# GpSimd's queue order between norm offsets and residual additions in a Strassen-Winograd SwiGLU block on Trainium2

## The reference, cut to what matters

```
xn = layernorm(x)                                  # rows of 1024
q, k, v = xn@Wq, xn@Wk, xn@Wv                      # 64 wide
g = sigmoid(xn@Wg + bg)
S = decay*S + (k*g) (v*g)^T ; o = q@S ; s = o@Wo   # recurrence over the rows
gate, up = xn@Wgate.T/127, xn@Wup.T/127            # 3072 wide
ffn = (silu(gate)*up) @ Wdown.T/127                # back to 1024
out = x + s * silu(ffn)
```

## Time and profile before

| what | value |
|---|---|
| time, median of the runs | 534.76 us |
| lowest time | 533.02 us |
| time of the profiled execution | 532.67 us |
| span of its slowest core, 6 | 531.1 us |
| spans of the others | 526.7 (core 4) to 530.3 us (core 3) |
| TensorE (PE) busy | 505.8 us, 95% of the span |
| VectorE (DVE) busy | 359.9 us, 68% |
| ScalarE (ACT) busy | 189.2 us, 36% |
| GpSimd (POOL) busy | 122.2 us, 23% |

### The profile page before, as it was taken

One profiled execution on the slowest core, in us unless ns is written; L12 is line 12 of the kernel. 1 busy time (PEld: TensorE's weight loads), 2 busy tenths in 40 slices (PEclk: granted clock), 3 DMA queues, 4 the chain that ended last, 5 costly groups with the idle time before them and its releaser, 6 DMA issues.

```text
span 531.1 us, 8803 instructions; the slowest of 8 cores (526.7 to 531.1 us)
## 1 busy us (share of the span) xinstructions
PE 505.8 (95%) x2722; PEld 240.1 (45%) x2722; DVE 359.9 (68%) x683; ACT 189.2 (36%) x296; POOL 122.2 (23%) x189
## 2 busy tenths in 40 slices
PE   4799989999999999968999999999999999999996
PEld 2455544445554444433555444444444444444442
DVE  4768666666777788976366667666666667967444
ACT  2523454454443321145621444333333333111111
POOL 3636312222327000434142531111111100000000
PEclk9999999999999999998999999999999999999999
DMA  7999999999999540485658995554454500032342
GB/s 214 223 123 161 160 163 157 122 155 140 146 161 193 98 141 2 122 246 173 187 165 199 170 180 81 93 84 74 78 90 75 85 10 0 1 120 99 120 138 79
DMA packets 37452, 66.77 MB, mean 126 GB/s; under 512 B 3295, under 2 KB 12639, under 8 KB 37408
## 3 DMA queue, kind: packets, MB, share of 16 engines
q0 software_dynamic: 18672, 36.19, 46.2%
q1 hardware_dynamic: 18592, 29.89, 17.8%
q10 hardware_dynamic: 144, 0.14, 0.1%
HBM read 89.28 MB, written 8.39 MB: 184 GB/s over the span
## 4 chain that ended last, share of the span: by engine, by line
PE 84%; DMA 5%; DVE 4%; issue 3%; POOL 2%; ACT 2%; SPq 0%; DVEq 0%; ACTq 0%; POOLq 0%
PE bank L465 50%; PE bank L521 24%; DMA xr<-xpfm 2%; PE bank L627 2%; DMA xs<-xtm 1%; DMA xr<-xtm 1%; ACT xnt_all L1133 1%; PE bank L646 1%; PE bank L533 1%; PE bank L609 1%; PE bank L457 1%; PE bank L447 1%; DVE sg_all L828 1%; POOL xr L1286 1%; DVE bst L851 1%
## 5 line engine op out<-in xcount | busy, mean ns | idle before, releaser
L465 PE MATMUL bank<-xs,S_w 128*128 128x512 f16 x552 | 139.8, 379 | 1.6 <-ACT bank L1174 1.6
L465 PE MATMUL bank<-xnT,gu 128*128 128x512 f16 x368 | 94.5, 379 | 0.0
L465 PEld LDWEIGHTS bank<-xs,S_w 128*128 128x128 f16 x552 | 52.0, 98 | 61.9 <-issue 1.7
L1211 POOL DMA_DIRECT2D gu<-wgu x48 | 26.2, 547 | 183.2 <-PE bank L465 174.7
L1048 DVE TENSOR_TENSOR bank<-bank,m 128x512 f32<-128x512 f32 x46 | 32.2, 699 | 51.0 <-PE bank L465 51.0
L465 PEld LDWEIGHTS bank<-xnT,gu 128*128 128x128 f16 x368 | 34.7, 98 | 40.0 <-issue 0.2
L733 DVE SCALAR_TENSOR_TENSOR hT<-bank,sg_all 128x512 f16<-128x512 f32 x69 | 47.1, 689 | 6.8 <-PE bank L465 5.7
L1056 DVE TENSOR_TENSOR m<-bank,m 128x512 f32<-128x512 f32 x46 | 31.8, 691 | 26.1 <-PE bank L465 25.7
L465 PE MATMUL bank<-xs,gu 128*128 128x512 f16 x184 | 47.3, 380 | 0.0
L465 PE MATMUL bank<-xnT,S_w 128*128 128x512 f16 x184 | 47.2, 379 | 0.0
L521 PE MATMUL bank<-wd,hT 128*128 128x512 f16 x192 | 45.3, 387 | 0.0
(11 more groups left out here) (158 smaller groups left out, 720.4 us busy)
## 6 DMA issues: line engine op xcount, KB each, us to landing
gu<-wgu POOLq DMA_DIRECT2D x96, 256.0 KB, 8.2
xr<-xtm SPq DMA_DIRECT2D x16, 512.0 KB, 5.0
out<-xr SPq DMA_DIRECT2D x32, 256.0 KB, 2.1
xs<-xtm SPq DMA_DIRECT2D x12, 512.0 KB, 4.2
wd<-wdt POOLq DMA_DIRECT2D x24, 256.0 KB, 11.7
xr<-xpfm POOLq DMA_DIRECT2D x8, 512.0 KB, 12.6
hT<-gu SPq DMA_DIRECT2D x5, 512.0 KB, 5.5
wd<-xtm SPq DMA_DIRECT2D x4, 512.0 KB, 15.7
```

What stands on the lines that cost most here:

```text
L465: mm = pe.matmul(out=out[:], lhsT=weight(d), rhs=moving(d), start=(start and d == 0), stop=(d == 3), skip_group_check=True)
L1211: g.dma_start(out=gu[idx % NGU][:, 0:1024], in_=wgu[idx % NHC][:, 0:1024]).then_inc(ld_gate[idx % NGU], 16)
```

## The change

- In `down_stage` each block's `dres` and `dst` go behind the `hooks` of their position, so that GpSimd takes `rs` and `nb` of the position ahead of the residual addition, and SyncE `x_load` ahead of the store.
- `dfin` (0,0) goes from behind `SD` (1,1) and (1,2) to its own product's place, behind `dsilu` (0,0). (4,0) stays where it was.
- `SD` (P+1,4) goes from behind `SD` (P+1,3) to behind `dfin` (P,3), one position later.
- Copy 0 is issued by ScalarE, ahead of `dsilu` (0,3). Copies 1 and 2 go behind `dst` (P,3) and both `res_load`, on SyncE.
- `norm` 8 and 9 go one position earlier. As the hooks are now appended in three loops, every `stats` of a position stands ahead of its `norm`, and each `norm` ahead of `tr` and `ev`.

```diff
-        p, group = P % 4, lambda n: [("dsilu", (P, n)), ("dfin", (P, n)), ("dres", (P, n)), ("dst", (P, n))]
+        p = P % 4
+        sums = lambda *which: [("SD", (P + 1, i)) for i in which] if p < 3 else []
+        tail = lambda n: [("dres", (P, n)), ("dst", (P, n))]
...
         elif m == 2:
-            out.append(("wo", (P, 0)))
-            out += [("dsilu", (P, 0))] if p == 0 else group(0)
+            out += [("wo", (P, 0)), ("dsilu", (P, 0))]
+            if P != 4:
+                out.append(("dfin", (P, 0)))
+                behind = tail(0)
         elif m == 7:
             out += [("wo", (P, 1)), ("addM", P)]
             if p == 0:
-                out += following + [("dfin", (P, 0)), ("dres", (P, 0)), ("dst", (P, 0))]
-            out += group(1)
+                out += sums(1, 2)
+            if P == 4:
+                out += [("dfin", (P, 0))] + tail(0)
+            out += [("dsilu", (P, 1)), ("dfin", (P, 1))]
+            behind = tail(1)
         elif m == 3:
-            out += [("wo", (P, 2))] + group(2)
-            if p < 3:
-                out += [("SD", (P + 1, 3)), ("SD", (P + 1, 4))]
+            out += [("wo", (P, 2)), ("dsilu", (P, 2)), ("dfin", (P, 2))] + sums(3)
+            behind = tail(2)
         else:
-            out += [("tcopy", P)] if P < 3 else []
-            out += group(3)
+            out += [("tcopy_act", 0)] if P == 0 else []
+            out += [("dsilu", (P, 3)), ("dfin", (P, 3))] + sums(4)
+            behind = tail(3)
             if P < 7:
-                out += [("res_load", 2 * P + 2), ("res_load", 2 * P + 3)]
-        out += hooks.get(k, [])
+                behind += [("res_load", 2 * P + 2), ("res_load", 2 * P + 3)]
+            if P in (1, 2):
+                behind += [("tcopy", P)]
+        out += hooks.get(k, []) + behind
...
     for j in range(8):
         hook(7 + j).append(("stats", 8 + j))
-        hook(9 + j).append(("norm", 8 + j))
+    for j in range(8):
+        hook(8 + j if j < 2 else 9 + j).append(("norm", 8 + j))
+    for j in range(8):
         if j < 4:
             hook(9 + j).append(("x_load", 12 + j))
...
+                elif stage == "tcopy_act":
+                    s.wait_ge(pe_dprod, dprod(0, 4))
+                    s.dma_start(out=bass.AP(hT, 0, [[NHC * NH, 128], [NH, 24], [1, 256]]),
+                                in_=TD_home(0, 2, 0, 12)).then_inc(ld_tc[0], 16)
```

More of the change, by code:

```diff
@@ L44, in down_stage @@
     for k, (P, m) in enumerate(DSEQ[28 * half:28 * half + 28]):
-        p, group = P % 4, lambda n: [("dsilu", (P, n)), ("dfin", (P, n)), ("dres", (P, n)), ("dst", (P, n))]
+        p = P % 4
+        sums = lambda *which: [("SD", (P + 1, i)) for i in which] if p < 3 else []
+        tail = lambda n: [("dres", (P, n)), ("dst", (P, n))]
         out.append(("dp", (P, m)))
-        following = [("SD", (P + 1, 1)), ("SD", (P + 1, 2))] if p < 3 else []
+        behind = []
         if m == 1:
@@ L56, in down_stage @@
             else:
-                out += following
+                out += sums(1, 2)
         elif m == 2:
-            out.append(("wo", (P, 0)))
-            out += [("dsilu", (P, 0))] if p == 0 else group(0)
+            out += [("wo", (P, 0)), ("dsilu", (P, 0))]
+            if P != 4:
+                out.append(("dfin", (P, 0)))
+                behind = tail(0)
         elif m == 7:
@@ L63, in down_stage @@
             if p == 0:
-                out += following + [("dfin", (P, 0)), ("dres", (P, 0)), ("dst", (P, 0))]
-            out += group(1)
+                out += sums(1, 2)
+            if P == 4:
+                out += [("dfin", (P, 0))] + tail(0)
+            out += [("dsilu", (P, 1)), ("dfin", (P, 1))]
+            behind = tail(1)
         elif m == 3:
-            out += [("wo", (P, 2))] + group(2)
-            if p < 3:
-                out += [("SD", (P + 1, 3)), ("SD", (P + 1, 4))]
-        else:
-            out += [("tcopy", P)] if P < 3 else []
-            out += group(3)
+            out += [("wo", (P, 2)), ("dsilu", (P, 2)), ("dfin", (P, 2))] + sums(3)
+            behind = tail(2)
+        else:
+            out += [("tcopy_act", 0)] if P == 0 else []
+            out += [("dsilu", (P, 3)), ("dfin", (P, 3))] + sums(4)
+            behind = tail(3)
             if P < 7:
-                out += [("res_load", 2 * P + 2), ("res_load", 2 * P + 3)]
-        out += hooks.get(k, [])
+                behind += [("res_load", 2 * P + 2), ("res_load", 2 * P + 3)]
+            if P in (1, 2):
+                behind += [("tcopy", P)]
+        out += hooks.get(k, []) + behind
     return out
@@ L1329, in _ @@
                     y.wait_ge(pe_dprod, dprod(i, 4))
-                    homes = ([(0, 12)], [(0, 4), (4, 4), (8, 1), (9, 1), (10, 1), (11, 1)],
-                             [(0, 4), (4, 4), (8, 4)])[i]
+                    homes = {1: [(0, 4), (4, 4), (8, 1), (9, 1), (10, 1), (11, 1)], 2: [(0, 4), (4, 4), (8, 4)]}[i]
                     for d, n in homes:
```

## The result

The changed kernel takes 546.82 us (median of 4 runs, 545.95 to 573.54) beside 534.69 us for the kernel before in the same comparison: a ratio of 1.0231, 95% interval 1.0203 to 1.0259. It is slower by a little over 2%. In some executions the cores of one die show a lower granted clock and a longer time (573.54 us here, 626.48 us before); the ratios leave those out. The forecast, 541.8 us, had the direction and 7 of the 12 us.

The account below looks back on a forecast made before the run. TensorE, busy 95% of the span, was taken as the bound, so only its pauses count. Core 3's span of 530.3 us plus 7.62 gives 537.9, plus 1.8 for the clock 539.7, plus 1.6 around it 541.3; said 541.8, range 536 to 547.5.

Parts of the forecast that it names:

- my own case: The forecast's main case, 541.8 us: chance 0.5, spread from 539.5 (clock holds) to 544 us (sums contended).
- the 545.4 that I gave 0.26: Outcome slower by over 2%, 545.4 us or more: chance 0.26.
- The ring: Norms 9 to 12: nb i behind rs i+2 makes engines work in turn; 9.50, 7.31, 7.31 us; core 6's transpose 13 5.87 later.
- Rival 1: GpSimd and SyncE stop holding up the norms, no ring binds: 523 to 531, say 528 us; chance 0.12.
- Rival 3: Ring shorter, as ev and VectorE's sum overlap the waits: 3.7 us less, 536.3 with clock at full rate; chance 0.15.
- The change wins: Faster outcome around the norms, pauses at the transposes gone: say 528 us; chance 0.12.
- the clock's 1.8: Slow stretch at 1.2 GHz after the last pause, at transpose 12: +1.8 us, or 0 if the clock holds.
- Core 3 has the largest loss that counts: Core 3, 0.90 us behind core 6 at wo (0,2), reaches transpose 13 7.62 us later; span 530.3 becomes 537.9.
- Hidden with 0.5 to 2.5 us to spare; price 0: Late copy 2 and loads ahead of dres (3,0): done by 295.24, when dsilu (3,3) wants it; price 0.
- rival 2: Ring binds and copy 2 lands late: TensorE's second product of the next half waits 3.9 us, 545.7 us; chance 0.2.
- my own signs of being wrong: nb 10 before 238, TensorE's pauses between 213 and 262 us shrinking, or a pause at product (3,4).
- `dfin` (0,0) and copy 0 on ScalarE, each booked at 0: First position: dfin (0,0) moved, 0 us, bounds -0.8 and +0.3; copy 0 on ScalarE, 0 us, bounds -0.3 and +0.3.

Follow-up runs that it names:

- b_new_hooks: Kernel before with only the change's hooks order (stats ahead of norm, norm ahead of ev, norm 8 and 9 sooner): 547.32 us, ratio 1.0155.
- a_old_hooks: Changed kernel with the hooks loops merged again, each norm ahead of the next stats, other moves kept: 540.38 us, ratio 1.0019.
- nb_with_rs: Two runs with nb i right behind rs i on GpSimd: in the kernel before 527.94 us, ratio 0.9859; in the changed kernel 529.55 us, ratio 0.9890.
- b_nb_with_rs: Kernel before with only nb i right behind rs i on GpSimd (chunks 8 to 15): 527.94 us, ratio 0.9859.
- b_copies_late: Kernel before with only copies 1 and 2 moved behind the pair's last store and both res_load: 541.33 us, ratio 1.0114.
- b_dfin00: Kernel before with only dfin (0,0) at its own product's place: 533.64 us, ratio 0.9966.
- a_old_copies: Changed kernel with copies 1 and 2 ahead of the pair's last block again: two comparable runs, 552.12 and 549.69 us, no ratio.

## Why the prediction was right, and where its size was off

- **Where the result lies.** 546.82 us is inside the range of 536 to 547.5, but close to its top: above the 544 up to which I let my own case spread, and above the 545.4 that I gave 0.26.
- **The ring** was right, term by term. `norm` 9 was to start 19.65 us after `wo` (0,1) (232.29 on core 6, where `wo` (0,1) was at 212.64); on core 1 it did, at 236.06 with `wo` (0,1) at 216.41. Forecast 9.50, 7.31 and 7.31 us between the norms 9 to 12, measured 9.77, 7.29 and 7.44 on core 1, 24.5 in all against 24.12. The pauses came where they were put: 6.36 us at transpose 10 (forecast 6), 2.49 at 11 and 4.24 at 12 (forecast 2.5 to 4 each). b_new_hooks makes it alone, a_old_hooks and both nb_with_rs undo it. Rival 1 needed VectorE at `stats` 12 before 235; it got there at 242.61 on core 1, which is 238.8 when counted like core 6 before, 3.8 us earlier. Rival 3, a shorter ring, fell too: `ev` and the sums stand in it in full.
- **"The change wins" held a truth.** `nb` 9 early took transpose 9's wait away, and b_nb_with_rs shows 1.4% to be had from that wait for all chunks. The change put a worse one in its place.
- **The terms of the sum.** The forecast carried core 3 from `wo` (0,1) at 213.53 us through 50.0 to transpose 13 (with the clock's 1.8) and 276.2 more: 539.7. The slowest core of the changed kernel passes `wo` (0,1) at 216.41, takes 51.1, and then 277.3: 544.8. The differences are 2.9, 1.1 and 1.1 us, the whole miss of 5.1 in the span.
- **The 2.9: "Core 3 has the largest loss that counts."** This step failed. When a core reaches `wo` (0,1), ahead of anything that the change does to TensorE, varies by some microseconds from core to core and run to run: 210.5 to 213.5 us before, 210.4 to 216.4 after, core 1 at 210.96 in the one and 216.41 in the other. These 5.4 us lie far ahead of the down part, whose first product starts at 193.47 and 198.91: in the run after, TensorE waits 2.23 us for ScalarE at 78.1 us, where core 1 had no such wait before, and its mean granted clock is 0.90 from 10 to 20 us, 0.97 to 40 and 0.93 from 80 to 100, where it was 1.00. Before, the slowest core was the one with the longest section (core 6, 48.6 us where six cores had 46.3 to 46.9). After, all sections but core 3's are 56.5 to 57.6, and the slowest core is the one that started last. I took the loss from core 6, whose section was the longest before, and from core 3, which had started last; the median core lost 10.8 us in the section, and the median span rose from 528.6 to 541.6.
- **The section's 1.1.** The ring is 0.4 longer than the sum of its terms, and the slow stretch behind transpose 12 costs 2.5 us (5.58 to the next transpose, 3.03 at full clock) and not 1.8. Three microseconds of it, in a window of core 1, stand at 1.2 GHz with TensorE busy throughout:

```profile
262.00:265.00 3.00, 3.00 (x14) 1.63 (x15) 0.00 (x0) 3.00 (x4) 0.85 (x4) 0.50 0.83 238
```
- **The last 1.1: "Hidden with 0.5 to 2.5 us to spare; price 0."** This step failed; it is rival 2's mechanism at part of its price (it forecast 3.9). On core 1, GpSimd, then SyncE:

```profile
304.44 0.57 POOL L1226 DMA_DIRECT2D gu<-wgu  x1 [16.89 <-DMA hT<-gu]
...
307.62 4.98 POOL L1301 TENSOR_TENSOR xr<-sg_all,xr 128x512 f32<-128x512 f32 x4
```
```profile
276.85 11.13 SPq L1341 DMA_DIRECT2D out<-xr  x4
288.08 7.10 SPq L1334 DMA_DIRECT2D xr<-xtm  x2
295.29 4.03 SPq L1347 DMA_DIRECT2D hT<-gu  x3
```
  Copy 2 is issued from 295.29 and there at 304.44; then come six issues of loads, then `dres` (3,0), and ScalarE's last silu, whose product ended at 307.65, starts at 309.05. TensorE waits 0.94 to 1.58 us on every core, and on cores 0, 6 and 7 another 0.31 to 1.06 at product (3,4). From the first of the two `res_load` to the landing of the copy I had allowed about 12 us; it was 16.4. The two loads, the second behind its wait for the store of (2,3), held the queue for 7.10 us where I had given them 4, and the three issues took 4.03 instead of 2.8. b_copies_late shows that without the ring's delay the same move costs 1.1%. A pause at product (3,4) was among my own signs of being wrong, and it is there on those three cores, though not on the slowest.
- **`dfin` (0,0) and copy 0 on ScalarE, each booked at 0.** The sum came out right by luck: from `wo` (0,1) to `wo` (1,0) core 1 takes 16.13 us before and 16.14 after. `dfin` (0,0) alone makes it 15.07 (b_dfin00), 1.06 less, where I had allowed 0.8. Copy 0's issue of 0.69 us makes `dsilu` (0,3) 0.79 us late, where I had allowed 0.3 for its effect, and with `SD` (1,4) behind that `dfin` it comes back as 1.04 us at `recur` 7. Copy 0, `dres` behind the hooks and the moved `SD` (1,4) were not run alone.

## What to carry to other kernels

Before moving a stage in a list that orders all engines, write down for each engine which stranger it now stands behind, and follow that until the path closes: `nb` i behind `rs` i+2 tied three in-order queues (ScalarE, VectorE, GpSimd) into one ring, 24.5 us where 11.5 were possible. A tiny instruction that only needs its own chunk goes right behind its own input. And where the metric is the slowest of several cores, take the loss from the median core and add the spread of the starts, rather than follow the core that was slowest in one profile.

## What the hardware showed unexpectedly

- VectorE's f16 sum of 128x1024, 0.68 us by itself, took 4.86 us beside three GpSimd additions back to back, until 0.56 us after the last of them, though its record starts 0.55 us before theirs (core 2 of a_old_copies). The pair of sums at 220.85 us in the changed kernel took 2.42 us, 1.02 without an addition beside it. The Trainium skill (SBUF — State Buffer, "SBUF: two separate sides") describes a lock held for a whole instruction; by that alone one addition of 1.26 us would have been the most to wait for. These rows show a wait over several. It isn't always so: on core 1 of the same run a sum beside two additions in a row (305.24 to 308.19 us) took 1.32 us and ended while the second ran.
- Waits of 2.25 us (b_copies_late), 4.24 and 6.36 us on TensorE were each followed by a stretch at 1.2 GHz, but those of 2.49 at transpose 11 on core 1 and of 2.58 at transpose 12 on core 3 by none (the 12 matmuls at 254.95 on core 1 took 2.75 us), while on core 3 one of 1.99 at transpose 11 was followed by such a stretch (12 matmuls took 4.06 us, at a mean granted clock of 0.59 from 250 to 253). So the length of the pause alone doesn't decide it, and what else does no run here tells.
- Copy 2, three issues of one size from SBUF to SBUF, held SyncE's queue for 2.77 us in the kernel before (core 1), 4.03 in the changed one and 10.64 in b_copies_late. A price taken from one place in the trace did not hold at the other.
- The kernel before took 539.36 us on one chip (mean clock of its cores 0.984) and 535.13 and 536.37 on two others (0.995 and 0.996), so the ratios above are all of one chip. The windows and sections, which compare traces of different chips, don't have that guard.
